# Attention sum, its norm and the last layer's transform in one stage of a four-layer graph network

## The reference, cut to what matters

```python
def layer0(h): W_r = sum_b w_comp[r, b] * bases[b]; msg = (h @ W_type32)[src] * norm       # 32 relations
def layer1(h): msg = (h @ W_type16)[src] * norm * sigmoid((h @ gate)[src])                  # 16 relations
def layer2(x):                                                                              # attention, 8 heads of 32
    h = (x @ W.T).reshape(n, 8, 32)
    alpha = leaky(a_src . h[src] + a_dst . h[dst] + relu(edge_attr @ edge_W.T + edge_b) . h[dst])
    ex = exp(alpha - segment_max(alpha, dst)[dst])
    attn = ex / max(segment_sum(ex, dst)[dst], 1e-10)
    return segment_sum(h[src] * attn, dst) + bias
def layer3(h): msg = (h @ W_type20)[src] * norm                                             # 20 relations
for layer in (0, 1, 2, 3):
    r = layer(x); x = layernorm(x + (r if layer == 2 else relu(r)))     # out of 0, 1, 3: segment_sum(msg, dst)
```

## Time and profile before

| what | us |
|---|---|
| median of three runs | 8360.5 |
| the profiled execution, its own time | 8366.55 |
| its span in the profile | 8364.7 |
| from the memset that ends "softmax" to the first instruction of "last" | 5406.04 to 7154.14 |
| "gather_sum" in it | about 5417 to 6364 |
| "norm" and the first weights' split | about 6364 to 6424 |
| two passes of layer 3 | about 6424 to 7154 |

### The profile page before, as it was taken

The page is one execution under the profiler, slowest core; times in us unless marked ns, Lnnn a source line. Parts: engine busy times, 40 slices in busy tenths (PEclk is TensorE's granted clock), DMA queues, the critical chain, the costliest instruction groups (busy, mean ns, idle before and its releaser), DMA issues. The chain is left out here.

```text
span 8364.7 us, 88481 instructions
## 1 busy us (share of the span) xinstructions
PE 5697.3 (68%) x20891; PEld 4066.0 (49%) x20892; DVE 3801.3 (45%) x9956; ACT 1686.8 (20%) x3167; POOL 3568.4 (43%) x3450
## 2 busy tenths in 40 slices
PE   5999996888886555555555555266665999555554
PEld 2878785666665333333333333134443878333333
DVE  2111113555554555544444445687776111444444
ACT  1444442333332000001111111100001444000000
POOL 0000003666665666665555555044341000566665
PEclk8999998999998767676676677577777999766666
DMA  5444444555554333334555556033332444333333
GB/s 163 187 186 186 172 188 158 185 186 187 186 181 145 109 107 108 108 109 145 189 186 189 189 187 199 34 117 122 114 124 105 186 172 186 115 98 95 98 96 94
DMA packets 395622, 1231.38 MB, mean 147 GB/s; under 512 B 101090, under 2 KB 169420, under 8 KB 355141
## 3 DMA queue, kind: packets, MB, share of 16 engines
q1 hardware_dynamic: 234645, 784.90, 25.1%
q0 software_dynamic: 160752, 443.96, 18.5%
HBM read 636.14 MB, written 592.41 MB: 147 GB/s over the span
## 5 line engine op out<-in xcount | busy, mean ns | idle before, releaser
L574 POOL DMA_INDIRECT ring<-table,idx x2496 | 2373.1, 951 | 3409.4 <-DVEq L813 1310.1
L1280 PE MATMUL ps<-W_r,work_r 128*128 128x512 f32 x7800 | 1842.4, 394 | 3.8 <-DVE work_r L716 3.8
L1297 PE MATMUL ps<-ring,W 128*128 128x256 f32 x3328 | 1132.8, 462 | 787.3 <-DVE A L806 420.6
L1280 PEld LDWEIGHTS ps<-W_r,work_r 128*128 128x128 f32 x7800 | 1454.5, 189 | 300.8 <-issue 5.8
L1297 PEld LDWEIGHTS ps<-ring,W 128*128 128x128 f32 x3328 | 676.7, 225 | 1173.0 <-issue 708.7
L788 DVE TENSOR_SCALAR W<-iota,dloc,norm 128x128 f32<-128x128 f32 x1664 | 589.1, 355 | 1166.0 <-PE ps L1297 585.7
L1129 ACT ACTIVATE A<-ps 128x512 f32<-128x512 f32 x1300 | 777.9, 598 | 1090.7 <-PE ps L1280 1090.7
L1297 PE MATMUL ps<-ring,A 128*128 128x256 f32 x1664 | 608.6, 507 | 438.9 <-DVE X L806 338.8
L712 DVE CAST work_r<-ps 128x256 fp32r<-128x256 f32 x250 | 106.0, 424 | 1525.2 <-PE ps L1269 1525.2
L1297 PEld LDWEIGHTS ps<-ring,A 128*128 128x128 f32 x1664 | 379.6, 251 | 643.0 <-issue 319.8
L806 DVE TENSOR_TENSOR X<-X,ps 128x256 f32 x1664 | 686.5, 413 | 8.8 <-PE ps L1297 4.6
(11 more groups left out here) (230 smaller groups left out, 5403.3 us busy)
## 6 DMA issues: line engine op xcount, KB each, us to landing
table<-A SPq DMA_DIRECT2D x300, 768.0 KB, 3.3
table<-A SPq DMA_DIRECT2D x200, 512.0 KB, 2.6
table<-A SPq DMA_DIRECT2D x98, 1024.0 KB
rows_dram<-ring SPq DMA_DIRECT2D x52, 1056.0 KB
rows_dram<-A SPq DMA_DIRECT2D x52, 1056.0 KB
ring<-rows_dram SPq DMA_DIRECT2D x52, 1056.0 KB, 4.9
W<-rows_dram SPq DMA_DIRECT2D x52, 1056.0 KB, 4.9
ring<-table,idx POOLq DMA_INDIRECT x2496
```

Of the source, the lines that this page charges most:

```text
L574: pool.indirect_dma_start(out=f_ring[:, s % NR, :], out_offset=None, in_=src, in_offset=bass.IndirectOffsetOnAxis(ap=idx[:, s:s + 1], axis ...
L1280: ins = pe.matmul(ps[:, b, :], rows[:, u, c, :], w[:, c, b * 512:(b + 1) * 512], start=(n == 0), stop=(n == len(terms) - 1))
L1297: pe.matmul(ps[:, s % banks, 0:D], marks_[:, s % G, :], f_ring[:, s % NR, :], start=True, stop=True).then_inc(wk.step_done, 1)
```

## The change

"gather_sum", "norm" and layer 3's two passes become one phase "sum", written as "fused" is: in slot k the steps of window k run, window p = k-1 is divided, added to x, normalised and transposed, and window q = k-2 is multiplied by all 20 relations in 10 banks.

```diff
-                   ("gather_sum", None), ("norm", 2)] + relational(p3, walk3)[:-1] + [("last", walk3)])
+                   ("sum", None), ("last", walk3)])
+        CH = 4
+        BANK_TICKS = [1 + b * 15 // (R3 * D // 512) for b in range(R3 * D // 512)]   # 1 2 4 5 7 8 10 11 13 14
+        s_acc = XF[:, 0:NW1 * GROW]...           # the accumulator takes X's place; x of layers 2 and 3 stays in memory
+        s_rows = [ring[:, c * CH:(c + 1) * CH, :] for c in range(U // CH)]           # 4 buffers of 4 steps
 PE:
+            def sum_products(_):
+                def step(s):
+                    c = s // CH
+                    if s % CH == 0:
+                        pe.wait_ge(s_marked, c + 1); pe.wait_ge(s_weighed, c + 1); pe.wait_ge(s_exp, c + 1)
+                    if s >= SB:                                                       # SB = 3
+                        pe.wait_ge(s_added, s - SB + 1)
+                    pe.matmul(ps[:, s % SB, 0:GROW], s_marks[:, s % (2 * CH), :], s_rows[c % 4][:, s % CH, :], ...)
+                for k in range(NW1 + 2):
+                    p, q = k - 1, k - 2
+                    for j in range(SLOT):
+                        s = k * SLOT + j
+                        if s < STEPS:
+                            step(s)
+                        if q >= 0:
+                            if j == 0:
+                                pe.wait_ge(s_xt_ready, q + 1)
+                                pe.wait_ge(s_w_low, S_BANKS)
+                            for b in range(S_BANKS):
+                                if j == BANK_TICKS[b]:
+                                    bank_products(q, b)       # waits for s_bank_free m - 3, six matmuls
+                        if 0 <= p < NW1 and j == 12:
+                            turn_row(p)                       # waits for f_normed
 POOL:
+            def clear(_):                                     # in "softmax"
+                pool.memset(XF[:, 0:NW1 * GROW], 0.0)
             def weigh(_):
+                for c in range(CHUNKS):                       # 208
+                    pool.wait_ge(s_row[c % 4], 16 * (c // 4 + 1))
+                    pool.wait_ge(s_ex_in[c % 4], 16 * (c // 4 + 1))
+                    pool.tensor_tensor(rows_, rows_, s_ex[:, c % 4]..., ALU.mult).then_inc(s_weighed, 1)
 DVE:
+            def mark(c):                                      # four steps in one instruction
+                dve.tensor_tensor(s_marks[four steps], iota[...].to_broadcast([P, CH, P]),
+                                  dloc[...].to_broadcast([P, CH, P]), ALU.is_equal).then_inc(s_marked, 1)
+            # slot: addition of step s; mark(c + 2) after each fourth; for window p: j 0 max, 1 reciprocal, 2 times the
+            # inverse, 3 plus x, 4 and 5 statistics, 8 reciprocal, 9 normalise, 14 and 15 high and low part;
+            # in slot 0, j 4 to 13: the low part of a weight bank each
 ACT:
+            # slot: copies the weights of chunk s//4 + 2 into its rows; j 7 square root; one tick after each bank of PE: its copy;
+            # in slot 0, j 3 to 12: the high part of a weight bank each
 SP:
-            def take_up(_): load(X[:, 0:NW1, :], x2_dram...)
+            def keep_ex(_):                                   # in "softmax"
+                sp.wait_ge(m_out, QM // BLK + 1)
+                load(ex_dram, W[:, NSC:2 * NSC])
+            # "sum": rows and weights of chunk c once chunk c - 4 is done; x rows per window; x3 rows out;
+            # table3 in two stores of five banks; ten loads of weight banks at the start, two buffers
 "last":
-                    dve.tensor_scalar(X[:, bass.ds(at, 1), :]..., f_xin, ...)        # reads x from X, writes X
+                    dve.tensor_scalar(last_acc[:, bass.ds(at, 1), :]..., f_xin, ...)  # x loaded from x3_dram per window
 all walks:
-                for s in range(KP):
+                for s in range(STEPS):
```

More of the change, by code:

```diff
@@ L539, in last_stores, with load_x @@
-                sp.dma_start(full[ROWS:P], X[ROWS:P, 0:NW1 - 1, :]).then_inc(stored, 16)
+                at = {}
+                def load_x(k):
+                    _, (reg,) = nc.values_load_multi_w_load_instructions(
+                        order[0:1, k:k + 1], engines=[sp.engine], min_val=0, max_val=NW1 - 1,
+                        skip_runtime_bounds_check_because="the order is a permutation of the windows")
+                    at[k] = reg
+                    g = 3 * NW1 + k
+                    sp.dma_start(f_xin[:, g % 2, :], x3_rows[bass.ds(at[k], 1)].squeeze(0)).then_inc(f_x_in[g % 2], 16)
@@ L540, in last_stores @@
+                load_x(0)
+                load_x(1)
+                for p in range(NW1):
+                    sp.wait_ge(f_normed, 3 * NW1 + p + 1)
+                    sp.dma_start(out[bass.ds(at[p] * P, ROWS), :], last_acc[0:ROWS, bass.ds(at[p], 1), :].squeeze(1)).then_inc(stored, 16)
+                    if p + 2 < NW1:
+                        load_x(p + 2)
+                sp.dma_start(full[ROWS:P], last_acc[ROWS:P, 0:NW1 - 1, :]).then_inc(stored, 16)
                 sp.wait_ge(stored, 16 * NW1 + 16)
-            run(sp, {"setup": setup, "weights": weights, "fused": fused_transfers, "gat": gat_transfers, "pass": store_table, "norm": norm_loads,
-                     "last": last_stores, "scores": spill, "softmax": take_up, "gather_sum": reload})
+            run(sp, {"setup": setup, "weights": weights, "fused": fused_transfers, "gat": gat_transfers, "pass": store_table, "sum": sum_transfers,
+                     "last": last_stores, "scores": spill, "softmax": keep_ex})
@@ L722, in copies @@
                 body(NWIN // 2 - 1, False)
-            def window_registers(i, h):
-                _, regs = nc.values_load_multi_w_load_instructions(
-                    win[0:1, bass.ds(i * U + h * G, G)], engines=[dve.engine], min_val=0, max_val=NWIN - 1,
-                    skip_runtime_bounds_check_because="a step's window counts windows that have begun, at most all of them")
-                return regs
-            def steps(width, weighed, onehot_ready, step_done, added, granted):
-                def build(s, j):
-                    dve.tensor_scalar(onehot[:, j, :], iota[:, :], dloc[:, s], norm[:, s] if weighed else None, ALU.is_equal,
-                                      ALU.mult if weighed else ALU.bypass).then_inc(onehot_ready, 1)
-                for j in range(G):
-                    build(slice(j, j + 1), j)
-                with dve.Fori(0, ITERS) as i:
-                    for h in range(2):
-                        regs = window_registers(i, h)
-                        for j in range(G):
-                            dve.wait_ge(step_done, i * U + (h * G + j + 1 + granted))
-                            build(bass.ds(i * U + (h * G + j + G), 1), j)
-                            dve.wait_ge(added, i * U + (h * G + j + G))
-                            a = acc[:, bass.ds(regs[j], 1), 0:width].squeeze(1)
-                            dve.tensor_tensor(a, a, ps[:, j, 0:width], ALU.add).then_inc(added, 1)
-                dve.wait_ge(added, KP + G)
-                dve.wait_ge(onehot_ready, KP + G)
             def register_of(table_, k, most):
@@ L1089, in softmax @@
                     ins.then_inc(m_out, 1)
-                ch(dve.memset(A[:, 0:NWIN * GROW], 0.0))
-            def gather_sum(_):
-                dve.sem_inc(b_added, G)
-                steps(GROW, False, b_onehot, b_done, b_added, RU)
-            run(dve, {"setup": setup, "fused": fused, "gat": gat, "split": split, "pass": copies, "last": last, "norm": residual_norm,
-                      "scores": scores, "softmax": softmax, "gather_sum": gather_sum})
+                dve.wait_ge(m_out, QM // BLK + 1)
@@ L1100, in _ @@
+            run(dve, {"setup": setup, "fused": fused, "gat": gat, "split": split, "pass": copies, "last": last,
+                      "scores": scores, "softmax": softmax, "sum": attention_sum})
         @block.scalar
@@ L1232, in _ @@
+            run(act, {"setup": setup, "fused": fused_copies, "split": split, "pass": evacuate, "last": last_deviations, "gat": gat_copies,
+                      "scores": scores, "softmax": softmax, "sum": sum_copies})
         @block.tensor
@@ L1458, in _ @@
             run(pe, {"setup": setup, "fused": fused_products, "pass": products, "last": last_products, "gat": gat_products,
[L1459 removed]
+                     "scores": scores, "softmax": softmax, "sum": sum_products})
 def kernel(**inputs):
```

348 lines of the change are left out of this document (232 added, 116 removed).

## The result

| | before | after |
|---|---|---|
| time, median of 4 runs | 8357.3 us (8353.5 to 8371.3) | 7760.4 us (7757.0 to 7765.8) |
| ratio | | 0.9284, 95% interval 0.9267 to 0.9300 |
| profiled execution: own time, span, clock | 8366.6, 8364.7, 0.802 | 7761.6, 7759.8, 0.814 |

The forecast was 7800 us. The changed kernel is 7% faster and 40 us better than forecast, inside the range of 7740 to 7970.

What follows compares the result with a forecast made beforehand. DVE, held up by POOL, bounds "gather_sum" and PE bounds layer 3's passes. 1190 us replace 1748.1 (558 saved), other phases save 7: 8366.6 - 558 - 7 = 7801.6, said as 7800 us, range 7740 to 7970.

Steps and rivals of the forecast that it cites:

- store of exponentials, on the path: Before the new phase, in the memset's place: storing 3.41 MB, 9.8 us at 349 GB/s and some 2 to land, 12 us.
- slots 0 and 1: Start of the new phase: slot 0 waits for ten weight banks, 45 us (35 to 60); slot 1 has none, 16 us.
- PE's work in a slot: In "sum": 17 steps of 0.454 us, ten banks of 1.39 and 0.3 for two transposes, 21.9 us.
- stall 0.8: At the slot's end, PE waits for DVE's late addition: nothing without mark or lock, some 2 us with one; 0.8 a slot.
- clock 0.3: In each slot of "sum": 0.3 us added for granted clock, as "fused" got 0.94 and the pass 0.98.
- 47 slots: Slots 2 to 48 of the new phase, at 23.0 us each: 1081 us.
- other phases: "fused", "gat" and "last" lose two padding steps each: at most 8.7 us saved, 7 taken.
- 14 us of DVE work a slot: DVE in "sum": 12.0 us of additions, marks and norm, plus 2.1 us of waiting on POOL's lock.
- the first: Rival for the slot: handing on between PE, DVE and ACT, or locks, make it 26.5 us; 7965 us in all; 18%.
- The second: Rival for the slot: transfers bound it at a 186 GB/s ceiling, 28.2 us; 8045 us in all; 7%.
- the third: Rival "slower": PE gets the low clock, 1.2 GHz, slot 41 us, kernel about 8680 us; 3%.
- the fourth: Rival for the slot: no overlap, PE waits at every chunk for late-weighed rows; slot 33.3 us, kernel 8285 us; 2%.

## Why the prediction was right

The mechanism was right, but for what PE's one wait in a slot is for, and each term can be set beside its measurement:

| term | forecast | measured |
|---|---|---|
| store of exponentials, on the path | 12 | 9.3 (5401.78 to 5411.10) |
| slots 0 and 1 (first mark to first bank at 5473.1) | 61 | 62 |
| PE's work in a slot | 21.9 | 21.8 |
| added to it: stall 0.8, clock 0.3 | 1.1 | 0.5 |
| 47 slots | 1081 | 1045 |
| slots 49 and 50 | 28.4 | 28.1 |
| from PE's end (6546.4) to "last" | 8 | 5.5 |
| other phases | -7 | -4 |
| idle time ahead of the old phase | not counted | -2.7 |

The 21.8 are 17 x 0.445 + 10 x 1.39 + 0.3, since two steps in a row took 5988.73 - 5987.84 = 0.89 us in the timeline after (weight loads):

```profile
5987.84 0.86 PEld L1562 LDWEIGHTS ps<-ring,targets 128*128 128x128 f32 x4
5988.73 0.41 PEld L1579 LDWEIGHTS ps<-W_r,work_r 128*128 128x128 f32 x2
```

The mis-sized term is what is added to each slot, 1.1 us forecast and 0.5 measured. Together with the shorter step, 22.3 in place of 23.0 us make 47 x 0.7 = 33 us. Another 3 come from the last slot, since there are only 830 steps: from the first bank of slot 48 to that of slot 49 are 12 steps in place of 17 and no wait, 19.5 us. That is 1081 - 1045 = 36 of the 40 us. What is added had two parts.

The clock's 0.3 us was nothing. The granted clock was 1.00 from 5473 to 6503 us, where PE was busy 98.7% of the time; in "fused", at 83%, it stayed 0.94, before and after alike. I had carried over a loss of the phase with more idle time.

The stall's 0.8 us is in the row of waits as 32.1 / 46 = 0.70. The place was named rightly: four steps without a bank, and DVE with an addition, the low part, an addition and a mark. What PE waits for was not. The prediction laid it on a late addition (SB = 3), and put it at nothing in six slots of ten and 2 us in four. PE waits for the low part, whose semaphore stands before step j = 1, so a wait stands in every slot: 0.49 us without a mark, 1.09 with one, near 2 only in two slots of 46. That the average came out near 0.8 is in part luck. Part of the wait is given back, as the load behind it takes 0.30 us and not 0.42: 21.8 + 0.70 - 0.12 = 22.4, beside 22.3 measured.

The rest is small and of both signs: the store of the exponentials (3 us) and the phase's end (2.5) were put too high and the old phase's idle time (2.7) was left out, while the other phases gave 3 us less than forecast and slots 0 and 1 took 1 us more.

The lock between POOL and DVE had been weighed with the Trainium skill's rule ("SBUF — State Buffer", section "Who interferes with whom"). The runs agree with it in what it says of two SBUF inputs: the new marks, which read two tensors of SBUF, reach 2.43 us beside a POOL instruction of 1.92 and 4.17 beside one of 3.65. The additions, with one SBUF input and one from PSUM, never pass 0.432 us in 830. The normalisation reads one tensor from SBUF and a scalar for each partition, and it is held up too, as the timeline of the changed kernel shows:

```profile
5974.83 2.08 DVE L826 TENSOR_SCALAR onehot<-onehot,moments 128x256 f32<-128x256 f32 x1
5974.85 1.92 POOL L674 TENSOR_TENSOR ring<-ring,work 128x1024 f32<-128x1024 f32 x1 [1.46 <-DMA ring<-rows_dram]
```

The same section of the Trainium skill names this kind among those that can enter a two-port mode and then contend. But L826 takes 408 ns in the median for 256 columns and L732 279 for 128, 1.0 ns for a column more, so neither row looks like two columns at a time. If they are outside that mode, the section's exception for one SBUF input does not hold for them: L826 is held up above, and L732, the old mark, reached 3741 ns. No run here shows the mode. The estimate of 14 us of DVE work a slot compares with 691.06 / 1030 x 22.3 = 15.0 busy.

The prediction drew from that section of the Trainium skill that only shorter POOL instructions and fewer marks relieve DVE. The marks' waiting bears that out: 270 us before, 234 with shorter instructions alone, 93 in the changed kernel with 208 marks in place of 840. No run had fewer marks alone. But this relief is not the gain of the change: shorter instructions alone gave 60 of 253 us in the kernel before, and in the changed kernel taking away nearly all of the lock gives 4 to 8 us, because a wait on DVE lies under a bank.

Of the rivals, the first (26.5 us a slot) fell: the slot without gathers has next to no surplus over PE's sum, so handing on between engines costs next to nothing in this form; that the 4.6 us in "fused" come from the gathers was not tested by itself. The second fell with 264 and 303 GB/s, the third with the clock of 1.00, and the fourth with waits for POOL and ACT that did not come from 5480 to 6500 us. How a slot looks in which steps and banks take turns is the run with all banks at the slot's end: 30.5 us, near the 33.3 worked out for the fourth, though PE waits for additions there and not for rows.

## What to carry to other kernels

When one phase waits for one engine and the next for another, put their work into one slot and first add up the fullest engine's instructions from the trace; here that sum held to 2%, and most of the gain came from spreading the long pieces evenly, 387 us of 600. Then look for the longest stretch with no long piece: here the one wait that was left sat there in all 46 slots, and moving each piece by a step or less removed most of it. Look also at where a wait stands in the code: this one stood a step ahead of the piece that needs it. The lock between two engines cost 253 us where DVE set the pace and next to nothing where a bank lay beside it, so measure such a lock by cutting the one engine's work in both kernels before reshaping its instructions.

## What the hardware showed that was not expected

- The chips differ by up to 12% for one kernel: before took 7563.6, 8364.5 and 8439.8 us on three of them. The difference lies in phases with gathers: "last" took 1208 us in the changed kernel's first profile and 1061 on the quickest chip.
- One core's queues held 303 GB/s for 800 us, with 0.87 of their time used, where the prediction had only a ten-microsecond stretch of 349 to go by the earlier trace rows.
- The weighing of four steps takes 1.92 us and of eight 3.65, one step 0.62: 0.43 us for each step and 0.18 for the instruction. The prediction's halving of 3.64 to 1.82 missed the fixed part.
- Two additions into the accumulator, one behind the other, start 0.64 us apart, and the trace has the second wait for the first; with another instruction between them, as at 5983.22 above, no such wait is seen. Seventeen in a row would be 10.9 us of a slot and not 5.8, an estimate.
